# A graph network layer: the first layer of its edge gates as two whole-array matmuls in place of four 64x64 tiles

## The reference: what is computed

```
gates    = ssp(edge_attr @ We1 + be1) @ We2 + be2        # 200000 x 64
gates    = gates * (1 - sigmoid(5 * (dist - 3.5)))
h        = ssp(concat(x[src], x[dst]) @ Wn1 + bn1) @ Wn2 + bn2
sums     = zeros(12500, 64).at[dst].add(h * gates)
new      = x + ssp(sums @ Ws1 + bs1) @ Ws2 + bs2
out      = layernorm(x + new)
```

## Time and profile before

| | |
|---|---|
| median of three runs | 2500.21 us (2497.41 to 2500.76) |
| span of the profiled execution, first to last instruction | 1988.8 us |
| not in the span (median less span) | 511.4 us |
| PE busy | 1737.7 us (87%), 16249 instructions |
| PE weight loads busy | 1328.7 us (67%) |
| ACT busy | 1532.1 us (77%) |
| POOL busy | 1484.7 us (75%) |
| DVE busy | 1285.6 us (65%) |
| DMA | mean 79 GB/s |
| mean granted TensorE clock | 0.949 of full speed |

### The profile page before, as it was taken

How to read it: one execution, slowest core, us unless ns; L and a number is a source line. 1 busy time by engine, 2 the same in 40 slices (tenths; PEclk the granted TensorE clock), 3 DMA queues, 4 the chain that set the end, 5 groups by cost and what they waited for, 6 DMA issues and landing times.

```text
span 1988.8 us, 53540 instructions
## 1 busy us (share of the span) xinstructions
PE 1737.7 (87%) x16249; PEld 1328.7 (67%) x16249; DVE 1285.6 (65%) x3512; ACT 1532.1 (77%) x3368; POOL 1484.7 (75%) x1572
## 2 busy tenths in 40 slices
PE   4699999898888988878889988998988898988987
PEld 3577777676666666666666766766666676766666
DVE  4578888666665655555656666666666666666666
ACT  3589999777777777777777788788777787787877
POOL 7777777777777777777777777777777777777773
PEclk7799999999999899999989999899999899999999
DMA  5433333333333333333333333333333233333331
GB/s 122 122 85 98 97 97 97 85 85 76 91 74 73 71 73 70 75 68 71 74 71 74 74 80 74 74 75 78 74 75 75 69 84 75 75 78 75 75 76 38
DMA packets 256432, 157.78 MB, mean 79 GB/s; under 512 B 45401, under 2 KB 227046, under 8 KB 256366
## 3 DMA queue, kind: packets, MB, share of 16 engines
q1 hardware_dynamic: 202652, 104.94, 18.2%
q0 software_dynamic: 50048, 51.35, 15.5%
q10 hardware_dynamic: 3666, 0.68, 0.2%
HBM read 146.94 MB, written 9.87 MB: 79 GB/s over the span
## 4 chain that ended last, share of the span: by engine, by line
POOL 57%; issue 22%; PE 11%; DVE 3%; ACT 2%; SPq 2%; DMA 2%; DVEq 1%; ACTq 1%; POOLq 0%
POOL ga L459 57%; PE ps L623 3%; PE ps L636 3%; PE ps L640 1%; DVE hid L1113 1%; SPq L340 1%; PE ps L585 1%; DMA ga<-in_x_dram,srcT 1%; PE ps L575 1%; DVE hid L1117 1%; PE ps L653 1%; PE ps L662 1%; PE ps L577 0%; DVEq L1139 0%; ACT lg L861 0%
## 5 line engine op out<-in xcount | busy, mean ns | idle before, releaser
L459 POOL DMA_INDIRECT ga<-in_x_dram,srcT x1564 | 1483.7, 949 | 477.6 <-issue 472.4
L852 ACT ACTIVATE lg<-ps,bn1c 128x512 f32<-128x512 f32 x391 | 268.4, 687 | 306.6 <-PE ps L585 267.6
L636 PE MATMUL ps<-wn,hid 128*128 128x64 f32 x3128 | 447.9, 288 | 18.9 <-DVE hid L1117 17.1
L1113 DVE SCALAR_TENSOR_TENSOR hid<-ps,neg_b,lg 128x512 f32<-128x512 f32 x391 | 292.8, 749 | 221.9 <-ACT lg L867 205.2
L636 PEld LDWEIGHTS ps<-wn,hid 128*128 128x128 f32 x3128 | 393.1, 197 | 51.5 <-DVE hid L1117 26.6
L575 PE MATMUL ps<-ident,ea 128*128 128x128 f32 x782 | 173.8, 305 | 198.2 <-DMA ga<-in_x_dram,srcT 135.2
L844 ACT COPY xe<-ps 128x512 f32<-128x512 f32 x391 | 229.9, 588 | 113.3 <-PE ps L577 99.8
L623 PE MATMUL ps<-xe,wn 64*128 64x256 f32 x1564 | 289.8, 449 | 0.0
L1151 DVE TENSOR_TENSOR acc<-acc,ps 64x64 f32 x782 | 168.4, 215 | 163.7 <-issue 157.9
L640 PE MATMUL ps<-we,hid 128*128 128x128 f32 x1564 | 273.1, 299 | 0.0
L575 PEld LDWEIGHTS ps<-ident,ea 128*128 128x128 f32 x782 | 80.0, 143 | 282.1 <-issue 268.8
(11 more groups left out here) (124 smaller groups left out, 1847.9 us busy)
## 6 DMA issues: line engine op xcount, KB each, us to landing
ea<-in_edge_attr_dram SPq DMA_DIRECT2D x195, 256.0 KB
ga<-in_x_dram,srcT POOLq DMA_INDIRECT x1564
bw<-b_tab SPq DMA_DIRECT2D x782, 32.0 KB
relb<-rel_tab SPq DMA_DIRECT2D x196, 64.0 KB
b_tab<-share SPq DMA_DIRECT2D x25, 250.0 KB
out_dram<-xs SPq DMA_DIRECT2D x25, 125.0 KB
xs<-in_x_dram SPq DMA_DIRECT2D x3, 750.0 KB
rows_i<-in_dst_dram SPq DMA_DIRECT2D x1, 768.0 KB
```

The source lines that it names most:

```text
L459: pool.indirect_dma_start(to[:, t % 2, t // 2, :], None, x, bass.IndirectOffsetOnAxis(ap=idx[:, t:t + 1], axis=0)).then_inc(done, 16)
L636: pe.matmul(hg[:, t * D:(t + 1) * D], hid[:, u % 2, t * P:(t + 1) * P], wn2[:, :], start=False, stop=False, skip_group_check=True)
L852: act.activation(lg[:, u % 2, 0:QUAD].rearrange("p (k e) -> p k e", k=2), z[:, :, 0:PAIR], ACT.Abs, bias=bn1c[:, 0:1]).then_inc(n_abs, 1)
L1113: dve.scalar_tensor_tensor(out=hid[:, u % 2, 0:QUAD].rearrange("p (k e) -> p k e", k=2), in0=ps[:, 2 * (u % 2):2 * (u % 2) + 2, 0:PAIR], s ...
```

## The change

The gates' first layer gets the form that the second has already. `we1` becomes [128, 128] with We1 twice on its diagonal, and `gates_in` is two matmuls with K = 128 and M = 128, one for each half k: out come both j at once, on partitions 64j to 64j+63 of bank k. Hidden gate values lie as [64j + d, k*128 + p]. So the second layer's two matmuls write 128 neighbouring columns each. ACT and DVE have the same instructions with the same shapes; only the names of the axes differ. The memset that clears `we1` has twice the columns, and its two loads write 64 columns of 64 partitions as before.

```diff
-        we1 = sb("we1", [P, D])
+        we1 = sb("we1", [P, P])
...
             def gates_in(u, slot):
-                for j in range(2):
-                    half = slice(j * D, (j + 1) * D)
-                    for k in range(2):
-                        mm = pe.matmul(ps[k * D:(k + 1) * D, 2 * (u % 2) + j, PAIR:PAIR + P], we1[half, :],
-                                       xe[half, slot, 0, k * P:(k + 1) * P], start=True, stop=True)
+                for k in range(2):
+                    mm = pe.matmul(ps[:, 2 * (u % 2) + k, PAIR:PAIR + P], we1[:, :], xe[:, slot, 0, k * P:(k + 1) * P],
+                                   start=True, stop=True)
                 return mm
...
-                gates = hg[:, PAIR:2 * PAIR].rearrange("p (k j d) -> p k j d", k=2, j=2)
-                for j in range(2):
-                    mm = pe.matmul(gates[:, :, j, :], hid[:, u % 2, QUAD + j * P:QUAD + (j + 1) * P],
-                                   we2[:, :].rearrange("p (k d) -> p k d", k=2),
-                                   start=False, stop=(j == 1), skip_group_check=True)
+                for k in range(2):
+                    mm = pe.matmul(hg[:, PAIR + k * P:PAIR + (k + 1) * P], hid[:, u % 2, QUAD + k * P:QUAD + (k + 1) * P],
+                                   we2[:, :], start=False, stop=(k == 1), skip_group_check=True)
                 mm.then_inc(hg_mm, 1)
...
-                act.dma_start(we1[half, :], We1).then_inc(ld_bd, 16)
+                act.dma_start(we1[half, half], We1).then_inc(ld_bd, 16)
...
-                act.activation(lg[:, u % 2, QUAD:QUAD + PAIR].rearrange("p (j e) -> p j e", j=2), z[:, :, PAIR:PAIR + P],
+                act.activation(lg[:, u % 2, QUAD:QUAD + PAIR].rearrange("p (k e) -> p k e", k=2), z[:, :, PAIR:PAIR + P],
                                ACT.Abs, bias=be1c[:, 0:1]).then_inc(e_abs, 1)
```

More of the change, by code:

```diff
@@ L1117, in hidden @@
                 dve.scalar_tensor_tensor(
-                    out=hid[:, u % 2, QUAD:QUAD + PAIR].rearrange("p (j e) -> p j e", j=2),
+                    out=hid[:, u % 2, QUAD:QUAD + PAIR].rearrange("p (k e) -> p k e", k=2),
                     in0=ps[:, 2 * (u % 2):2 * (u % 2) + 2, PAIR:PAIR + P], scalar=neg_b[:, 1:2],
-                    in1=lg[:, u % 2, QUAD:QUAD + PAIR].rearrange("p (j e) -> p j e", j=2), op0=ALU.max, op1=ALU.add).then_inc(hid_b, 1)
+                    in1=lg[:, u % 2, QUAD:QUAD + PAIR].rearrange("p (k e) -> p k e", k=2), op0=ALU.max, op1=ALU.add).then_inc(hid_b, 1)
             def message(q, u, hg, scattered=sc_mm):
```

## The result

| device time, us | median | lowest to highest | runs |
|---|---|---|---|
| before | 2498.81 | 2491.53 to 2500.76 | 4 |
| changed | 2531.03 | 2521.86 to 2550.39 | 4 |

The ratio is 1.0124 with a 95% interval of 1.0092 to 1.0157: the change costs 32 us. The forecast was 2502.1 us, in a range of 2493 to 2509: wrong. One thing has to be known to read the numbers: the same program has two regimes, about 1993 and about 2500 to 2540 us, and the profile of before shown above was taken in the shorter one, all the timed runs beside it in the longer. That is what the experiments found; the profile after was taken in the longer one.

A forecast was written before the change was run, and what follows sets the result against it. POOL's gathers, 4.99 us per step of four, were taken to bound the kernel and hide PE's added work except +1.9 us at the end: 2500.2 + 1.9 = 2502.1 us, range 2493 to 2509 us.

The forecast's parts named there:

- The bound: Whole loop: POOL's gathers set the pace at 4.99 us per step; PE needs 4.26, so has 0.7 us slack.
- The count of the ring: POOL's gather ring: quad 24's first gather needs quad 9's transposes, leaving POOL 23 us in hand at its closest.
- The part outside the trace: The 511.4 us by which the runs' median exceeds the profile's span, taken as unchanged by the change.
- The group's own price: Gates' first layer on PE: pitch from 0.38 to 0.59 us, +0.21 us per step, bounds -0.19 to +0.60.
- The second layer's cost of nothing: Gates' second layer, result in one run of columns in place of two: no cost, within 0.04 us per step either way.
- What of it lies on the path: In the 381 steps before the end POOL's gathers hide the added 0.21 us; only the end pays, +1.9 us.
- the term at the end: Last ten gates' groups: 9 x 0.21 less PE's 0.23 us wait, plus 0.21 in the last front: +1.9 us.
- (a): Rival: PE sets the pace in the timed runs, every step pays: +82 us, or +184 at lower clock; 4 in 100.
- (b): Rival: PE sets the pace in the timed runs and the whole-array group is cheaper: -74 us, 2426 us; 2 in 100.
- (c): Rival: POOL's gather pace shifts, at most 14 us; with half, 7 us, 2493 or 2507 us; 4 in 100 each way.
- (d): Rival: the end falls out otherwise as gather landings differ: +5 us (2505) or +0.2 us (2500.4); 20 in 100.
- (e): Rival: the order of PE's work moved, so other steps would be priced; given no chance.

The follow-up runs named there:

- e16: Kernel before with all four gathers from quad 16 on, each of 32 rows in place of 128: 1873.72 us, beside 1993.21 us for the kernel before.
- e17: The changed kernel, unchanged, run once more in the short regime: 1993.59 us, 1.0001 times the kernel before beside it.
- e18: Kernel before with the four 64x64 matmuls of the gates' first layer done twice, in the short regime: 1992.16 us, 0.9993 times the kernel before.

## Why the prediction was wrong

**The bound.** Here it failed: "POOL is never doing anything else" and "PE has 0.7 us of slack in every step", and with them "the cost of these steps is nothing". All are true of the trace that was read, and e16, e17 and e18 show them by experiment. They are not true of the timed runs, in which POOL's step is 6.1 us because its fourth gather is followed by a wait for PE's transposes, 563 us in all in the new profile of before. In them the change costs 32 us. (The count of the ring is off by one, to the safe side: L471 asks for q-15 quads transposed, the last of them quad q-16, so quad 24 needs quad 8.)

**The part outside the trace.** "I take that part, which the trace does not show, as unchanged" is the sentence that let it through. A span of 1988.8 us against a median of 2500 was a fifth of the time, and an execution takes its span and 2 us. The trace spoke for another regime than the one whose time was asked for.

**The group's own price.** Predicted 0.59 us pitch and +0.21; measured 0.55 (1958.38 - 1957.83) and +0.17. At the lower clock it was to be 1.10; the changed kernel's timeline in the long regime has 1.02 against 0.63:

```profile
1211.34 1.22 PE L583 MATMUL ps<-xe,we 128*128 128x128 f32 x4
1212.36 0.55 PE L575 MATMUL ps<-ident,ea 128*128 128x128 f32 x2
```

The row shows 0.17 us more where the Trainium skill's rule on packing ("TensorE: Matmul & The Clock Gate", Part 3) gave 0.38: right in its sign, too large here. A net gain, which the Trainium skill's rule on switches of the tiling mode ("TensorEngine Tiling (Array Packing)", Key Properties) would allow, does not appear. Whether a switch is a part of the old group's 0.38 us these rows can't tell: two passes at the new group's 0.14 us would be 0.28. The second layer's cost of nothing holds (1.0016, with its interval from 1.0002).

**What of it lies on the path.** Nothing was said to, but for +1.9 us at the end. In the short regime it was +0.4 us, with an interval from -1.4 to +2.0; with e18, where twice the work cost nothing, the term at the end looks too large, though the interval of the change holds it. PE's instructions are 14685 as forecast, its gather wait there 115.1 us where some 105 were expected, and the step without wait 4.06 us (1961.89 - 1957.83) where 4.15 were. In the long regime the group is paid in the loop. From the starts of L852 in the profiles of both kernels, a plain step (110 to 200) goes from 6.11 to 6.29 us and a step of the node phase (214 to 366) from 6.14 to 6.29, while steps 20 to 92, with the table of products, stay at 6.1. This overstates it: the profiles' spans differ by 44 us, the medians by 32, since the profiled execution of the changed kernel was the longest of its four.

**The rivals.** (a), that PE's work counts in every step of the timed runs, with 4 in 100, was the one that came true, for the reason that I gave it: 511 us unexplained. Its price, 82 us at full clock, was too high: 32 us, 0.08 per step in place of 0.21. "A PE step would have to be 2 us longer than the trace shows" was its condition, and it is: 6.1 against 3.94. But the mechanism was other: not more work on PE, but a PE that advances only as POOL's gathers let it. No row of the trace that was read pointed there; the 4 in 100 rested on the unexplained 511 us alone. (b) needed a cheaper group, which it isn't; (c) had gathers change their duration, and they keep it (946 and 949 ns); (d), by which only +0.2 us would be left at the end, fits the short regime's +0.4 as well as the forecast does; (e) didn't happen.

**What stays open.** What of a gather instruction holds PE back, and what of PE it holds: its matmuls, the loading of its instructions, or its signals. The records don't tell, since their starts run ahead of the signals. In the preamble a lack of instructions isn't it, since PE starts within 0.14 us of ACT's signals. Open too is what decides the regime. Kernels run beside each other shared it, and one chip has shown both; nothing in the program sets it. And in the long regime the kernel before took 2502 us on some occasions and 2537 on others. No version beat the kernel before: the pauses and memsets tried here cost as much as they won or more, and a gather that takes the rows of two with one instruction wasn't tried.

## What to carry to other kernels

Before anything is read from a profile, compare its span with the timed median: where they differ by more than a few us, the trace may be of another regime, and slack that it shows may not exist in what is timed. Where a wait is called "issue", look in the timeline which engine finished just before it ended. An engine that isn't always busy may still be the bound through what its instructions do to another; halving their number, with the bytes kept, shows it. Where both regimes can occur, a change has two prices, here 32 us and nothing, and each needs its own run of the kernel before beside it.

## What was unexpected of the hardware

- One program took 1993 us (30 runs, 1990.8 to 1998.2) or 2500 to 2540 us (all other runs, 2491 to 2546), with nothing in between.
- In the longer regime, 64 gathers issued back to back, 1.25 us each, stretch the exchange between PE's transposes and ACT's copies to four per some 10 us, from eight per 2.5 us; PE answers ACT within 0.14 us, ACT gets PE's groups some 20 us after their record.
- There, half of the gather instructions takes 28% off the time with the same bytes moved, and a quarter of the rows with the same instructions takes off nothing.
- There, the engine that takes PE's result started a median of 3.6 us after PE's recorded start, and 0.5 us in the shorter regime, while PE itself started 0.06 us after the end of what it waited for.
- A gather of 32 rows takes 0.87 us, one of 128 rows 0.95: most of it is the instruction, not its rows.
